# The passage from layer 1 to layer 2 of a four-layer graph network: pieces of two layers interleaved, on one core

## What is computed

```python
# layer 1
q, k = split(x @ W_qk.T);  v = x @ W_v.T
w = sum((q @ k.T / 8) * adj, axis=-1)          # a score per node
w = softmax(w, axis=nodes)                      # over the 128 nodes of a graph
x = layernorm(x + w * v)
# layer 2, K = 3
Xw = x @ Wv + bv;  sj, si = Xw @ aw[:d], Xw @ aw[d:]
T = adj * exp(leaky_relu(sj[None, :] + si[:, None] + ab))
T = T / sum(T, axis=-1)
H = x @ Wk[0] + T @ x @ Wk[1] + T @ T @ x @ Wk[2] + sum(bk)
x = layernorm(x + relu(H))
```

## Time and profile before

| what | us |
|---|---|
| three runs | 684.12, 682.32, 684.05; median 684.05 |
| profiled execution | 684.61 |
| its span (first to last instruction) | 682.8 |
| TensorE busy in the span | 630.0 |
| mean granted clock of TensorE | 0.977 of full speed |

### The profile page before, as it was taken

One profiled execution on the slowest core, in us unless ns is written; L12 is line 12 of the kernel. 1 busy time (PEld: TensorE's weight loads), 2 busy tenths in 40 slices (PEclk: granted clock), 3 DMA queues, 4 the chain that ended last, 5 costly groups with the idle time before them and its releaser, 6 DMA issues.

```text
span 682.8 us, 15857 instructions
## 1 busy us (share of the span) xinstructions
PE 630.0 (92%) x5014; PEld 457.3 (67%) x5014; DVE 562.5 (82%) x1712; ACT 525.1 (77%) x1191; POOL 378.1 (55%) x448
## 2 busy tenths in 40 slices
PE   5989999999999999879999789999999997999993
PEld 4667777777777776556666556675766664787883
DVE  3799998888888887768999959898998887588886
ACT  4557888877777777758888667787787785799995
POOL 1134556665555555746777514443445353798993
PEclk9999999999999999989999899999999998999997
DMA  9591338464636322544665333545454443478783
GB/s 275 164 231 47 78 63 219 84 147 89 145 84 170 74 33 32 92 94 91 86 100 98 61 63 78 109 87 101 92 99 90 98 89 63 79 175 182 177 195 124
DMA packets 174466, 76.14 MB, mean 112 GB/s; under 512 B 122160, under 2 KB 173872, under 8 KB 174384
## 3 DMA queue, kind: packets, MB, share of 16 engines
q1 hardware_dynamic: 164208, 66.34, 42.1%
q0 software_dynamic: 8448, 8.39, 8.4%
q10 hardware_dynamic: 1728, 0.40, 0.3%
HBM read 28.97 MB, written 8.39 MB: 55 GB/s over the span
## 4 chain that ended last, share of the span: by engine, by line
PE 23%; POOL 10%; DVE 9%; ACT 7%; DMA 6%; issue 5%; SPq 0%; ACTq 0%; POOLq 0%; DVEq 0%
PE banks L86 7%; PE banks L87 6%; PE banks L88 6%; POOL l_rstd L1069 4%; ACT x_resident L1078 4%; DMA xT_lo<-x_halves 3%; POOL x_halves L1130 3%; DMA l_TT_lo<-l_T_lo 3%; DVE l_st L1044 2%; POOL l_U L1960 1%; PE banks L1553 1%; POOL l_T_lo L1757 1%; ACT l_wexp L1279 1%; ACT l_t L1590 1%; DVE l_wn L1335 1%
## 5 line engine op out<-in xcount | busy, mean ns | idle before, releaser
L1078 ACT ACTIVATE x_resident<-l_pre,l_nmr,l_rstd 128x256 f32<-128x256 f32 x256 | 141.0, 607 | 18.1 <-POOL l_nmr L1072 18.1
L973 POOL TENSOR_TENSOR hq<-hq 128x512 f32<-128x512 f32 x48 | 69.5, 1448 | 96.9 <-ACT hq L690 94.6
L1130 POOL TENSOR_TENSOR x_halves<-x_resident,x_halves 128x1024 f16<-128x1024 f32 x46 | 98.1, 2134 | 3.9 <-ACT x_halves L1123 3.2
L1044 DVE BATCH_NORM_STATS2 l_st<-l_pre 128x6 f32<-128x256 f32 x256 | 93.3, 410 | 0.0
L86 PE MATMUL banks<-Wk_lo,xT_hi 128*128 128x258 f16 (+1 forms) x256 | 84.4, 330 | 1.5 <-DVE l_far_lo L1708 0.8
L1069 POOL TENSOR_TENSOR l_rstd<-l_veps,minus_half 128x4 f32<-128x4 f32 x64 | 74.2, 1160 | 18.3 <-DVE l_veps L1058 15.0
L87 PE MATMUL banks<-Wk_hi,xT_lo 128*128 128x258 f16 (+1 forms) x256 | 84.3, 329 | 0.0
L88 PE MATMUL banks<-Wk_hi,xT_hi 128*128 128x258 f16 (+1 forms) x256 | 84.2, 329 | 0.0
L86 PE MATMUL banks<-W2T_lo,h_hi 128*128 128x257 f16 x256 | 71.0, 277 | 5.3 <-ACT zf L702 3.9
L87 PE MATMUL banks<-W2T_hi,h_lo 128*128 128x257 f16 x256 | 71.0, 277 | 0.0
L88 PE MATMUL banks<-W2T_hi,h_hi 128*128 128x257 f16 x256 | 70.9, 277 | 0.0
(11 more groups left out here) (200 smaller groups left out, 1943.1 us busy)
## 6 DMA issues: line engine op xcount, KB each, us to landing
adj<-in_adj SPq DMA_DIRECT2D x32, 256.0 KB, 3.5
x_halves<-in_x SPq DMA_DIRECT2D x16, 512.0 KB, 4.4
x_resident<-b_half SPq DMA_DIRECT2D x8, 1024.0 KB, 7.4
x_resident<-in_x POOLq DMA_DIRECT2D x16, 512.0 KB, 6.1
out<-x_resident SPq DMA_DIRECT2D x15, 512.0 KB, 3.2
x_resident<-in_L_gnn_W SPq DMA_DIRECT2D x2, 512.0 KB, 5.5
x_resident<-in_L_gnn_Wk SPq DMA_DIRECT2D x1, 768.0 KB, 9.4
xT_hi<-x_halves SPq DMA_TRANSPOSE x48, 3.2
```

Of the source, the lines that this page charges most:

```text
L973: pool.tensor_tensor(hq[:, 0, :], hq[:, 0, :], hq[:, h, :], ALU.add).then_inc(hqs_ok, 1)
L1044: dve.bn_stats(L.st[p][:, j, :], L.pre[p][:, j, :]).then_inc(L.st_ok, 1)
L1078: act.activation(K.x[:, gcols(g, j)], L.pre[p][:, j, :], ACT.Identity, bias=L.nmr[p][:, j:j + 1], scale=L.rstd[p][:, j:j + 1]).then_inc(L. ...
L1130: pool.tensor_tensor(F.xs[p][1], x_group(K, g), F.xs[p][0], ALU.subtract).then_inc(F.x_lo, 1)
```

## The change

It writes the border of layers 1 and 2 in another order on four engines (SP's string stays). No instruction is added or taken out. The last steps of layer 1 are cut into more steps, group 0's first pieces of layer 2 get steps of their own (lead 4 on TensorE, 3 on ScalarE and VectorE, instead of 1, 2, 2), and the strings mix them. Moved on TensorE: the fourth projection of group 15 behind three far products; far product 3, the spread, near products 0 and 1 in between the small pieces of group 15; near products 2 and 3 behind three far products of group 1, far product 3 of group 1 behind near product 3. On ScalarE the exponentials of group 15 come behind layer 2's first exp, the norms of group 13 and 14 behind that and around T_high, those of group 15 behind the whole of ScalarE's round 0. On VectorE the four far low halves come ahead of group 15's scores, T ahead of its residuals. On POOL T_low comes ahead of group 15's scale factors, and these ahead of the low halves of x group 2. The first residual of layer 2 waits for group 13's new x only, that of group 14 for all.

```diff
-SEAMS_PE = ('nonn', 'ooooon', 'oon')
-SEAMS_ACT = ('nnnonn', 'ooonononn', 'ooonnnonn')
-SEAMS_DVE = ('oononn', 'oooon', 'nonn')
-SEAMS_POOL = ('ooooo', 'ooon', 'ooonnn')
+SEAMS_PE = ('nonn', 'onononono', 'oon')
+SEAMS_ACT = ('nnnonn', 'nononono', 'ooonnnonn')
+SEAMS_DVE = ('oononn', 'onono', 'nonn')
+SEAMS_POOL = ('ooooo', 'onno', 'ooonnn')
...
@@ layer 1, tensor: step @@
+            if g == G + 1:
+                project(G - 1, 1, 3)
+            if g == G + 2:
+                aggregate(G - 1, 1)
+            if g == G + 3:
+                score_rows(G - 1, 1)
+            if g == G + 4:
+                weight_columns(G - 1, 1)
+        return step, 0, 5
...
@@ layer 1, scalar: step @@
+            if g == G - 1:
+                copy_qkv(G - 1, 1, 3)
+            if g == G:
+                exponentials(G - 1, 1)
+                norms(G - 3, 1)
+            if g == G + 1:
+                norms(G - 2, 0)
+            if g == G + 2:
+                norms(G - 1, 1)
+        return step, 2, 3
...
@@ layer 1, vector: step @@
+            if g == G + 1:
+                scores(G - 1, 1)
+                norm_row(L, dve, G - 2, 0, 0)
+                norm_row(L, dve, G - 2, 0, 1)
+                minimum(G - 1, 1)
+                norm_row(L, dve, G - 2, 0, 2)
+                norm_row(L, dve, G - 2, 0, 3)
+                softmax(G - 1, 1)
+                norm_variance(L, dve, G - 2, 0, EPS)
+            if g == G + 2:
+                residuals(G - 1, 1)
...
@@ layer 2, tensor: step @@
-            if has(1):
+            if has(1) and g >= 0:
                 project_far(g + 1, q, 0)
                 project_far(g + 1, q, 1)
                 project_far(g + 1, q, 2)
+            if g == 0:
+                project_near(0, 0, 2)
+                project_near(0, 0, 3)
+            if has(1) and g >= 0:
                 project_far(g + 1, q, 3)
...
+            if g == -4:
+                project_far(0, 0, 0)
+                project_far(0, 0, 1)
+                project_far(0, 0, 2)
+            if g == -3:
+                project_far(0, 0, 3)
+            if g == -2:
+                spread(0, 0)
+                project_near(0, 0, 0)
+            if g == -1:
+                project_near(0, 0, 1)
+        return step, 4, 1
...
@@ layer 2, scalar: step @@
+            if g == -1:
+                T_high(0, 0)
...
+            if g == -3:
+                far_halves(0, 0, (0, 1, 2))
+            if g == -2:
+                far_halves(0, 0, (3,))
...
+            if g == -2:
+                weights(0)
...
@@ layer 2, vector: residual and step @@
             if j == 0 and is_first(g):
+                dve.wait_ge(K.x_new[1], (G - 2) * GP)
+            if j == 0 and g == G - 2:
                 dve.wait_ge(K.x_new[1], G * GP)
...
+            if g == -3:
+                far_low(0, 0, 0)
...
+            if g == -2:
+                transition(0, 0)
+                row_sums(0)
+                normalised(0)
```

More of the change, by code:

```diff
@@ L1240, in step @@
             q = 1 - p
-            if has(-1):
+            if has(-1) and g < G:
                 project(g - 1, q, 3)
-            if has(-2):
+            if has(-2) and g <= G:
                 weight_columns(g - 2, p)
@@ L1285, in step @@
                 high_half(g + 3, q)
[L1286 to L1290, removed]
+            if has(-2) and g < G - 1:
+                norms(g - 2, p)
             if has(1):
                 copy_qkv(g + 1, q, 0)
-            if has(0):
+            if has(0) and g < G - 1:
                 exponentials(g, p)
@@ L1307, in residual, with residuals @@
                                      K.x[:, gcols(g, j)], ALU.mult, ALU.add).then_inc(L.pre_ok, 1)
+        def residuals(g, p):
+            residual(g, p, 0)
+            residual(g, p, 1)
+            residual(g, p, 2)
+            residual(g, p, 3)
         def scores(g, p):
@@ L1344, in step @@
             q = 1 - p
[L1345 to L1350, removed]
+            if has(-2) and g <= G:
+                residuals(g - 2, p)
+            if has(-1) and g < G:
                 scores(g - 1, q)
             once(g, 0, ones, 0)
-            if has(-2):
+            if has(-2) and g < G:
                 norm_row(L, dve, g - 2, p, 0)
                 norm_row(L, dve, g - 2, p, 1)
-            if has(-1):
+            if has(-1) and g < G:
                 minimum(g - 1, q)
-            if has(-2):
+            if has(-2) and g < G:
                 norm_row(L, dve, g - 2, p, 2)
@@ L1563, in step @@
                 walk_mid(g - 1, q, 3)
-            if has(0):
+            if has(0) and g > 0:
                 project_near(g, p, 0)
@@ L1604, in bias, with far_halves, weights @@
                            scale=1.0 / WK_SCALE).then_inc(S.s_bias, 1)
+        def far_halves(g, p, graphs):
+            for j in graphs:
+                bias(g, j)
+                far_high(g, p, j)
+        def weights(g):
+            logits(g, 0)
+            logits(g, 1)
+            logits(g, 2)
+            logits(g, 3)
+            exponentials(g)
         def mid_high(g, j):
@@ L1635, in step @@
                 norm_apply(K, L, act, g - 2, p, 2)
[L1636 to L1644, removed]
+            if g == -3:
+                far_halves(0, 0, (0, 1, 2))
+            if g == -2:
+                far_halves(0, 0, (3,))
+            if has(1) and g >= 0:
+                far_halves(g + 1, q, range(GP))
             if has(-2):
@@ L1651, in step @@
                 mid_high(g, 3)
[L1652 to L1658, removed]
+            if g == -2:
+                weights(0)
+            if has(1) and g >= 0:
+                weights(g + 1)
+        return step, 3, 2
     def vector(dve):
@@ L1742, in step @@
                 residual(g, p, 2)
-            if has(2):
+            if has(2) and g > -2:
                 far_low(g + 2, p, 0)
```

36 lines of the change are left out of this document (24 added, 12 removed).

## The result

The changed kernel's median is 676.89 us (675.47 to 680.02, 7 runs); the kernel before, run beside it on the same chip, has 682.57 (681.05 to 684.12, 7 runs). The ratio is 0.993, 95% interval 0.9909 to 0.9951: faster, by 4.8 us as the ratio gives it and by 5.7 between the medians. Forecast were 4.5 us less and an absolute time of 679.5 in 677.8 to 682.3.

The account below looks back on a forecast made before the run. TensorE, 92% busy, was taken to bound the kernel, with idle and slow time between layers 1 and 2. First walk 403.53 to 398.8 gives 4.7, less 0.25: 4.5 us, bounds 3.6 and 5.2; time 679.5, range 677.8 to 682.3.

Parts of the forecast that it names:

- The base: Time the gain is taken from: profiled 684.61 becomes 680.1, less 0.56 for the median of the runs shown, 679.5.
- Where the end is set: Layer 2's first walk, at 403.53 before: layer 2 then repeats without a gap, so whatever this walk gains should stay.
- TensorE's layout: Passage from layer 1 to 2, new order laid out with old durations: first far product at 381.86, weights ready at 390.1.
- T_hi 5.9 earlier: ScalarE, round 0 of layer 2: T_hi starts at 393.2 instead of 399.14.
- The lock, 1.1 us: VectorE's residuals of group 15 against T_lo on POOL: one residual can wait, bounds 0 and 1.3 us, taken as 1.1.
- The last wait: Ahead of the first walk: low half and far product 3 release it at 398.8; T's transpose, landing at 397.5, is not last.
- T_hi(1) slips 0.3 us: ScalarE, round 1 of layer 2: group 15's norms delay T_hi(1) about 0.3 us against the walk; 0.25 taken off the gain.
- rival 2: Round 1: T_hi(1) slips by the whole of the norms (2.06), next walk 1.8 later, 681.3; chance 0.10.
- The clock: TensorE in the passage: most old far products run at half speed; in the new order granted clock 1.00 from 380 to 395.
- rival 1: Clock falls in TensorE's lulls inside the new passage, losing 1.7 to 3.4 us, in the middle 2.5: 682.0; chance 0.15.
- rival 3: TensorE at 1.2 GHz through the whole passage: walk at 407.3, 3.8 late, 687.8; chance 0.04.
- Rival 4: The walk moves, but a wait no row shows, in round 1, eats the gain: no change, 684; chance 0.09.

Follow-up runs that it names:

- experiment 3: Changed kernel with POOL's T_lo of group 0 waiting until VectorE has finished group 15's residuals; 679.21 us against 681.27 for the kernel before, ratio 0.9951.
- experiment 7: Changed kernel plus 16 tiny, unread matmuls in each of eight rounds of layer 1; 675.83 us, a single run.
- experiment 8: Changed kernel unaltered, a third time; 676.95 us against 680.71 for the kernel before, ratio 0.994.
- experiment 1: Changed kernel run again unaltered; 677.19 us against 681.27 for the kernel before, ratio 0.9935.
- experiment 5: Experiment 4's order plus 9 idle 512-column matmuls in the lull before group 15's turned weights; 676.55 us against 680.71 for the kernel before, ratio 0.9933.
- experiment 6: Changed kernel plus 24 tiny, unread matmuls ahead of group 14's turned weights; 677.60 us against 681.05 for the kernel before, ratio 0.9951.
- experiment 4: Changed kernel with near products 0 and 1 of group 0 put back behind group 15's turned weights; 679.40 us, ratio 0.9966 to the kernel before.
- experiment 2: Kernel before with idle 512-column matmuls behind group 15's key sums (5) and turned scores (8); 683.57 us, ratio 1.0026 to the kernel before.

## Why the forecast gain came and the forecast time did not

**The base failed first.** The step is this one: "The profiled execution took 684.61, so it becomes 680.1; the median of the runs shown is 0.56 lower, so 679.5." The three runs shown had a median of 684.05. Four more of the same job brought it to 682.57, and three later jobs gave 681.27, 681.05 and 680.71. The base was 1.5 to 3.3 us too high. A gain of 4.5 taken from 682.57 gives 678.1. Of the 2.6 us between 679.5 and 676.89 the base makes 1.5; the other 1.1 is the difference of the medians, 5.7 instead of 4.5, and this is within the noise, since the interval of the ratio means 3.3 to 6.2 us. The range had the same fault: its low end is called "5.2 gained, and a median as low as the lowest run shown", but 682.32 - 5.2 is 677.1; 677.8 is what a gain of 4.5 leaves. It took in one of the two uncertainties where both were needed, and even 677.1 lies above 676.89.

**Where the end is set: right, as far as the profiles resolve it.** From the first walk to layer 3 it took 173.59 us before, and 173.41, 174.34 and 173.84 in the three profiles of the changed kernel. From the turned weights of group 14 to layer 3 they are 3.6, 2.9 and 4.7 us ahead of the one profile before.

**TensorE's layout: right.** First far product at +0.32, as forecast (381.86), turned weights of group 15 at +8.62, where the weights had been forecast ready at 390.1, which is +8.56. Small slips in the chain behind it (the sum to ScalarE's last high half is 397.3, VectorE's end with T_lo's term 397.8, and the handoff of rows 6 and 7 is 0.08 us) are 0.1 us or less.

**T_hi 5.9 earlier: right**, 6.06.

**The lock, 1.1 us: right in cause, near in size.** 0.98 us of the residuals is T_lo's (experiment 3), all of it in the one residual that met T_lo. The Trainium skill (SBUF — State Buffer, Who interferes with whom) had said that one side waits for a whole instruction and only one side; the traces agree, with 2.66 against 1.68 on VectorE and T_lo's 1.16 unchanged on POOL. Which of the two was issued first they do not settle: the records of that residual and of T_lo start at 390.59 and 390.61.

**The last wait: right in two profiles, wrong in four.** The layout put the walk at 398.8, +17.26, held by far product 3 behind the low half; experiments 7 and 8 have +17.05 that way. But "the T transpose lands at 397.5, no longer last" took the 2.5 us of one landing as a constant. In the profile after, and in experiments 1, 5 and 6, a completion came 1.6 to 2.6 us late and held the walk by 0.33 to 1.34 us. In the changed kernel it leaves 3.4 to 3.6 us of gain instead of 4.9. In the profile after, the walk's place, +18.56, is 400.1 on the old time axis, just over the 400 that was to show the forecast wrong. The ratios of the three measurements of the changed kernel (0.993, 0.9935, 0.994, so 4.8, 4.4 and 4.1 us) lie between. That the forecast 4.5 agrees with them is in part luck: its path, undisturbed, gives 4.9 less the 0.2 of the first round, and how often a fetch takes some of it away is not known from three profiles.

**T_hi(1) slips 0.3 us: right**, 0.23, and the first round is 0.18 longer (11.08 instead of 10.90); rival 2 is out.

**The clock: right for the new kernel, wrong about the old.** It stays at 1.00 from wn14 to the walk, through waits of 1.85 and 0.70 us, so rivals 1 and 3 did not come in any profile of the changed kernel. Rival 1 came in a variant: in experiment 3 the clock fell at the walk and cost 1.6 us in the round behind it, where 1.7 had been the price of the shorter fall. Experiment 4's fall lies in a lull that rival 1 had not named, that of group 15's softmax, which the near products fill in the changed kernel; its price was 2.1 us by experiment 5 and 2.5 by experiment 7, where 3.4 had been put for a fall of that length. But the prediction began with the half speed of the old far products as a part of the cost (from 385.4 to 392.2 by the trace's list, 0.3 us earlier than it read). Experiment 2 shows that it was none, since ScalarE's norms hid it. The sum had not used it, so the number did not suffer.

**Rival 4**, that it does not bind, is out: the intervals of all three measurements of the changed kernel end below 0.997.

## What to carry to other kernels

Count what an edit moves from the last point where both orders are the same, and take the absolute time from many runs of the base, not from three: here the difference was forecast within its noise and the base was off by up to three microseconds. A stretch at half clock is worth what waits for it and no more; look first at who evicts its results. Work put into a lull before a critical chain may be worth its cycles only as what keeps the clock up, and a DMA that lands one microsecond before it is wanted is not safely hidden.

## What the runs showed of the hardware

- A transpose whose 15 completions came in time had its 16th 1.6 to 3.0 us later in 5 of 11 profiles, each time with a 16 KB instruction packet of 0.9 to 1.4 us beside it (landing 4.1 to 5.4 us instead of 2.4 or 2.5). The same kernel showed it in two profiles and not in a third. Over all 13 profiles, a last completion over 0.5 us late was seen in 46 of 241 transposes with an instruction packet beside their end, and in none of 1423 without. The Trainium skill (DMA: Bandwidth & Descriptors, Queues, rings and completion order) says that the increment of the semaphore is an ordered write, which lands only after every earlier write from that DMA engine, across its queues. That would let a fetch hold a completion back; no view here shows whether both were on the same engine, and no run forced it.
- The granted clock fell to 1.2 GHz about a TensorE wait of 1.94 us in the kernel before, within one of 2.18 in experiment 4 and behind one of 2.74 in experiment 2, each time for 6.8 us; and in experiment 3 about the last of three waits of 0.87, 1.31 and 1.18, for some 3.4 us. It did not fall at 1.85 and 0.70 (profile after, experiments 1, 6, 7 and 8). So the length of one wait alone does not tell whether it falls.
- Where the clock falls outside the passage varies between runs of one kernel. The turned weights of group 14 came at 378.36, 379.89 and 382.22 us in the three profiles of the changed kernel.
